# Cross-attention and gated feed-forward on one core: the last projections reordered over four PSUM banks, and the second group of first-layer weights loaded in the last units

## What is computed

```
x = x + tanh(g_xattn) * (attention(layer_norm(layer_norm(x)), ctx, mask) @ w_proj + b_proj)    # 16 heads of 32, 128 keys
x = x + tanh(g_ffn) * ffn(layer_norm(x))
ffn(h): y = silu(layer_norm(h) @ w1 + fc1_bias);  h + 0.5 * (y @ w2 + fc2_bias)                # 512 -> 2048 -> 512
w1 = (fc1_q - 128) * fc1_scales    (per group of 128 rows; w2 the same from fc2_q, fc2_scales)
```

## Time and profile before

| | |
|---|---|
| median of 3 runs | 1099.59 us (1096.32 to 1099.66) |
| the profiled execution | 1091.72 us, its span 1089.9 us |
| TensorE busy | 1030.1 us, 95% of the span |
| VectorE busy | 648.7 us, 60% |
| ScalarE, GpSimd busy | 398.8 us, 329.1 us |
| attention block | from 0 to 400.15 us |
| feed-forward block | from 400.15 us to the end |

### The profile page before, as it was taken

One profiled execution on the slowest core, in us unless ns is written; L12 is line 12 of the kernel. 1 busy time (PEld: TensorE's weight loads), 2 busy tenths in 40 slices (PEclk: granted clock), 3 DMA queues, 4 the chain that ended last, 5 costly groups with the idle time before them and its releaser, 6 DMA issues.

```text
span 1089.9 us, 15131 instructions
## 1 busy us (share of the span) xinstructions
PE 1030.1 (95%) x5182; PEld 561.6 (52%) x5182; DVE 648.7 (60%) x1071; ACT 398.8 (37%) x612; POOL 329.1 (30%) x338
## 2 busy tenths in 40 slices
PE   5787999999989797999999999999999999999998
PEld 3455767767767453444444444444444444444443
DVE  5678989889877767785344435335346345335322
ACT  3467777877767622341121121121121121121111
POOL 4456667667756332202101102102102102012000
PEclk9889999999999999999999999999999999999999
DMA  7575777777766679202002002001000100200101
GB/s 277 126 206 160 218 196 213 221 225 200 215 171 173 203 221 343 91 1 78 1 1 78 1 1 77 1 1 42 37 1 31 47 1 1 78 1 1 39 1 39
DMA packets 61473, 109.38 MB, mean 100 GB/s; under 512 B 9656, under 2 KB 10848, under 8 KB 60896
## 3 DMA queue, kind: packets, MB, share of 16 engines
q1 hardware_dynamic: 58632, 104.11, 31.4%
q10 hardware_dynamic: 2776, 4.40, 1.3%
HBM read 72.57 MB, written 33.55 MB: 97 GB/s over the span
## 4 chain that ended last, share of the span: by engine, by line
PE 57%; DVE 3%; issue 1%; DMA 1%; ACT 1%; DVEq 0%; SPq 0%
PE ps_z L1428 9%; PE ps_z L1427 9%; PE ps_z L1429 9%; PE ps_y L238 9%; PE ps_y L239 9%; PE ps_y L240 9%; PE ps_h L1441 1%; DMA s_raw<-in_L_ffn_fc_scales 1%; DVE w_f L192 1%; ACT w_hi L183 1%; DVE x_in L1521 0%; DVE y_hi L1490 0%; DVE w_lo L195 0%; DVE x_stats L1543 0%; DVE x L1513 0%
## 5 line engine op out<-in xcount | busy, mean ns | idle before, releaser
L1464 ACT ACTIVATE y_f<-ps_y,cols,ffn_scales 128x512 f32<-128x512 f32 x128 | 99.3, 776 | 490.3 <-PE ps_y L240 490.3
L1490 DVE TENSOR_SCALAR y_hi<-y_f,ffn_scales 128x512 f16<-128x512 f32 x128 | 70.1, 548 | 331.4 <-ACT y_f L1464 331.4
L1427 PE MATMUL ps_z<-w_hi,y_hi 128*128 128x512 f16 x512 | 194.8, 381 | 7.0 <-DVE w_lo L195 7.0
L238 PE MATMUL ps_y<-ht_hi,w_hi 128*128 128x512 f16 x512 | 194.1, 379 | 1.5 <-PEq L278 1.5
L1428 PE MATMUL ps_z<-w_lo,y_hi 128*128 128x512 f16 x512 | 194.8, 381 | 0.0
L1429 PE MATMUL ps_z<-w_hi,y_lo 128*128 128x512 f16 x512 | 194.6, 380 | 0.0
L240 PE MATMUL ps_y<-ht_hi,w_lo 128*128 128x512 f16 x512 | 194.1, 379 | 0.0
L239 PE MATMUL ps_y<-ht_lo,w_hi 128*128 128x512 f16 x512 | 194.1, 379 | 0.0
L1492 DVE SCALAR_TENSOR_TENSOR y_lo<-y_f,ffn_scales,y_hi 128x512 f16<-128x512 f32 x128 | 103.2, 806 | 4.6
L773 ACT ACTIVATE p_f<-ps_s,fill_col 128x512 f32<-128x512 f32 x128 | 86.2, 673 | 4.0 <-PE ps_s L604 3.5
L775 ACT ACTIVATE p_hi<-ps_s,fill_col 128x512 f16<-128x512 f32 x128 | 85.4, 667 | 0.0
(11 more groups left out here) (203 smaller groups left out, 1606.6 us busy)
## 6 DMA issues: line engine op xcount, KB each, us to landing
q_pack<-q_dram SPq DMA_DIRECT2D x96, 256.0 KB, 4.0
q_dram<-q_hi SPq DMA_DIRECT2D x32, 256.0 KB, 3.3
q_dram<-q_lo SPq DMA_DIRECT2D x32, 256.0 KB, 3.7
x_dram<-x_out SPq DMA_DIRECT2D x32, 256.0 KB, 4.8
x_res<-in_x SPq DMA_DIRECT2D x28, 256.0 KB, 4.7
q_raw<-in_L_ffn_fc_q SPq DMA_DIRECT2D x6, 1024.0 KB, 10.7
s_raw<-in_L_ffn_fc_scales SPq DMA_DIRECT2D x6, 1024.0 KB, 13.9
x_in<-in_x SPq DMA_DIRECT2D x4, 1024.0 KB, 7.7
```

The costliest lines, as they stand in the source:

```text
L238: nc.tensor.matmul(out, s_hi, m_hi, start=(k == 0), stop=False)
L1427: nc.tensor.matmul(ps_z[t][:, :], hi, w2_hi[:, f, :], start=(f == 0), stop=False)
L1464: nc.scalar.activation(y_f[f % 2][:, :], ps_y[f % 2][:, :], ACT.Silu, bias=b1_c[:, f:f + 1], scale=y_unscale).then_inc(y_f_ready, 1)
L1490: nc.vector.tensor_scalar(y_hi[f % 4][:, :], y_f[f % 2][:, :], y_scale, None, ALU.mult).then_inc(y_hi_ready, 1)
```

## The change

**Loads.** `load_w1(1)` moves from the SyncE queue at the start of `feed_forward` to the ScalarE queue in step 34 of attention, between `weights_hi(0, 0)` and `weights_hi(0, 1)`. For this the raw tiles have names by group, and the integers of groups 1 and 3 have a tile each (`q1_second`, `q1_last`).

**Projections.** In step 31 `project(26, first)`, and in step 32 both halves of tile 27, stand ahead of `weighted_values`. Tiles 28 to 31 have a bank each (`ps_xp`, `ps_qm`, `ps_s[0]`, `ps_s[1]`) and all run in step 33: four first halves, then four second halves. The sums of tiles 30 and 31 go to `xt_f` and not to `x1_out`.

```
+            q1_second = sb("q1_second", [P, KB, GROUP * P], I32, first)
...
+            s1_raw, q1_raw = [s1_even, s1_odd, s1_even, s1_odd], [q1_even, q1_second, q1_even, q1_last]
...
+        def summed(i, k):
+
+            return xt_f[k % 2][:, :] if last_tiles(i, k) and k % KB >= 2 else x1_out[k % 2][:, :]
+
         def proj_bank(i, k):
 
-            return ps_qm if not real(i, k + KB, UNITS) and k % 2 else ps_xp
+            return ps_xp if real(i, k + KB, UNITS) else (ps_xp, ps_qm, ps_s[0], ps_s[1])[k % KB]
...
-                    after(pe, x1_ready, tile if real(i, k + KB - 1, UNITS) else tile - 1)
+                    after(pe, x1_ready, tile if real(i, k + KB, UNITS) else UNITS - KB)
...
+                if isinstance(i, int) and PER * i + k >= UNITS - 1 and real(i, k - 5, UNITS - KB):
+                    project(i, k - 5, first)
+                if isinstance(i, int) and PER * i + k >= UNITS and real(i, k - 5, UNITS - KB):
+                    project(i, k - 5, second)
                 if real(i, k - 1, UNITS):
                     weighted_values(i, k - 1)
...
                 if real(i, k - 5, UNITS) and not real(i, k - 5 + KB, UNITS):
-                    if k % 2:
+                    if PER * i + k == UNITS + 1:
                         for blocks in (first, second):
-                            project(i, k - 5, blocks)
-                            project(i, k - 4, blocks)
+                            for t in range(KB):
+                                project(i, k - 5 + t, blocks)
                     return
...
+                if u == UNITS + 2:
+                    g("load_w1")(act, 1)
...
-                    load_w1(sp, 1)
```

More of the change, by code:

```diff
@@ L104, in build @@
         maxima = [sb(f"maxima{n}", [P, TT, HG], F32) for n in range(2)]
+        GROUP = 4
         ffn_scales = sb("ffn_scales", [P, D], F32)
@@ L112, in build @@
             xt_lo = [sb(f"xt_lo{n}", [P, KB, CHUNK], F32R, rows32) for n in range(2)]
[L116 to L119, removed]
+        ht_hi, ht_lo = [sb("ht_hi0", [P, KB, CHUNK], F16)], [sb("ht_lo0", [P, KB, CHUNK], F16)]
+        with ExitStack() as first:
+            q1_second = sb("q1_second", [P, KB, GROUP * P], I32, first)
+        ht_hi.append(sb("ht_hi1", [P, KB, CHUNK], F16))
+        ht_lo.append(sb("ht_lo1", [P, KB, CHUNK], F16))
         w_f = [sb(f"w_f{n}", [P, 2 * D], F32) for n in range(2)]
@@ L175, in w_parts @@
                 held = slice(2 * n % GROUP, 2 * n % GROUP + 2)
-                parts = [w2_hi[:, blocks, :], w2_lo[:, blocks, :], s2_raw[group % 2][:, held, :], q2_raw[group % 2][:, held, :]]
+                parts = [w2_hi[:, blocks, :], w2_lo[:, blocks, :], s2_raw[group][:, held, :], q2_raw[group][:, held, :]]
                 full = w_f[at % 2][:, :].rearrange("p (f d) -> p f d", f=2)
@@ L487, in step @@
                     after(sp, x1_ready, PER * i + tile + 1)
-                    sp.dma_start(target, x1_out[t % 2][:, :]).then_inc(x1_stored[t % 2], 16)
+                    sp.dma_start(target, summed(i, tile)).then_inc(x1_stored[t % 2], 16)
                 if k == -1:
@@ L677, in step @@
                 if real(i, k - 5, UNITS) and not real(i, k - 5 + KB, UNITS):
-                    if k % 2:
+                    if PER * i + k == UNITS + 1:
                         for blocks in (first, second):
-                            project(i, k - 5, blocks)
-                            project(i, k - 4, blocks)
+                            for t in range(KB):
+                                project(i, k - 5 + t, blocks)
                     return
-                if real(i, k - 5, UNITS):
+                if real(i, k - 5, UNITS) and not (isinstance(i, int) and PER * i + k >= UNITS - 1):
                     project(i, k - 5, first)
@@ L686, in step @@
                     scores(i, k, 2)
-                if real(i, k - 5, UNITS):
+                if real(i, k - 5, UNITS) and not (isinstance(i, int) and PER * i + k >= UNITS):
                     project(i, k - 5, second)
@@ L927, in add_residual @@
                 after(dve, res_biased, tile + 1)
-                if real(i, k - 2, UNITS):
+                if real(i, k - 2, UNITS) and not (last_tiles(i, k) and k % KB >= 2):
                     after(dve, x1_stored[k % 2], 8 * (tile - k % 2))
-                nc.vector.tensor_tensor(x1_out[k % 2][:, :], proj_bank(i, k)[:, :], residual(i, k), ALU.add).then_inc(x1_ready, 1)
+                nc.vector.tensor_tensor(summed(i, k), proj_bank(i, k)[:, :], residual(i, k), ALU.add).then_inc(x1_ready, 1)
             def row_stats(i, c, tiles=range(TT)):
```

24 lines of the change are left out of this document (12 added, 12 removed).

## The result

The changed kernel is slower by half a per cent, in line with the forecast:

| | median (range), us | runs | ratio to before, 95% interval |
|---|---|---|---|
| before | 1095.61 (1091.39 to 1099.66) | 12 | 1 |
| after | 1100.83 (1098.9 to 1105.75) | 12 | 1.0051 (1.0035 to 1.0068) |

A forecast was written before the change was run, and what follows sets the result against it. TensorE, busy 95% of the span, was taken as the bound; only its idle time could move. Terms 3.1 + 1.8 - 3.6 + 2.8 gave +4.1 us, 1103.7 against the median 1099.6; range 1098.0 to 1108.5.

The forecast's parts named there:

- The load saves 3.6 us: Start of feed-forward: VectorE's 3.58 us wait for the group 1 scales goes entirely; bounds 3.6 us and 0.
- 0 to 0.6 us, and I take 0: VectorE's wait for all stores ahead of its first `y_hi`: the loss from stores sharing DMA engines with the load.
- The halves ahead cost 3.1 us at tile 28: End of attention: projections ahead of the weighted values wait for additions, so tile 28 starts at 390.20, not 387.11.
- Predicted idle times: TensorE idles 3.0, 2.7, 3.5 and 3.7 us ahead of 372.12, 382.70, 390.20 and the feed-forward.
- 3.7 us: End of attention: net loss before load and later clock terms come off, +3.7 us, without any slow stretches in either kernel.
- The last stretch costs 1.8 us: Tiles 28 to 31: tile 29 completes after the 36th matmul, not the 24th, so the last addition ends 1.8 us later.
- The clock costs 2.8 us, two slow stretches of three: Tile 27, last projections, first hidden products: two of three get 1.2 GHz, 1.4 us each; bounds 0 and +4.2 us.
- Clock stays high: Rival: clock stays high behind the three later idle times, or drops behind one only: +1.3 to +2.7 us; chance 0.31.
- Halves fill the idle time: Rival: halves of tiles 26 and 27 fill TensorE's idle time, tile 28 starts 2.1 us sooner: -3.9 us; chance 0.05.
- The load brings nothing: Rival: VectorE waits as long for the load or another transfer: +7.7 us, 1107.3; chance 0.08.

The follow-up runs named there:

- the load alone: The kernel before with only the load of first-layer group 1 moved to step 34 of attention, projections as before: ratio 1.0018.
- Own banks: The changed kernel with tiles 26 and 27 projected into `ps_qm` and `ps_max[0]`, and tile 28 not waiting for tile 27's addition: ratio 0.9976.
- four banks alone: The kernel before with only tiles 28 to 31 over four banks and the last two sums in `xt_f`; load at its old place: ratio 1.0007.
- the filler: The changed kernel with 12 matmuls that nobody reads added behind the last projections: ratio 1.0038.
- the load with sums in `xt_f`: The kernel before with the load moved and the last two sums in `xt_f`; projections in pairs, no halves ahead: ratio 0.9967.
- the last three kernels: Own banks with both weight conversions ahead of the last four sums: half of tile 27 ahead, both halves, or both with tile 29's sum in `p_f[1]`: 0.9947, 0.9947, 0.9942.
- the last timeline: VectorE's rows for Own banks with both halves of tile 27 ahead and both weight conversions right behind tile 27's addition: ratio 0.9947.

## Why the prediction was right, and where it was off

**The load saves 3.6 us: right against the profile of before, wrong in what it needs.** The wait for the load went in every kernel with the load ahead. With the last sums out of `x1_out` and a fast start of the feed-forward the gain was 3.6 us (0.9967). By itself the load gained nothing (1.0018). The step that failed is "0 to 0.6 us, and I take 0" for the stores: I asked only whether VectorE's wait for all stores ahead of `y_hi` would grow, and not whether the additions would wait for a free `x1_out`. With the load alone they lost 2.30 - 1.05 + 3.77 = 5.0 us, of which 3.77 are shown to be the load's. In the changed kernel this stayed hidden, because its last two sums go to `xt_f` and its tile 29 comes late. The Trainium skill, DMA: Bandwidth & Descriptors (Issuing engines are not separate DMA queues), has the rule that was weighed there, that loads on ScalarE's queue run on the same 16 engines as the stores. The trace agrees: the store of tile 29 took 7.9 us to land beside the moved load, and 2.3 without it. A second thing the sum left out: it took the whole 3.58 us and a slow start of the feed-forward besides. The two hide each other. Where that start is slow, the wait for a load at its old place is only 1.14 or 1.17 us.

**The halves ahead cost 3.1 us at tile 28: right, 3.66 measured.** The mechanism stands row by row. Predicted idle times were 3.0, 2.7, 3.5 and 3.7 us; the trace has 2.95, 2.96, 3.48 and 3.65. `weighted_values(30)` start 4.37 us behind `p_lo` (3 to 4 were forecast), tile 28 at 393.60 less the 2.83 us of the ruler, 390.77, against 390.20. Own banks show that the bank wait is the cause: with it gone the same order of instructions starts `weighted_values(31)` 6.9 us sooner on the ruler, even 1.1 us ahead of the kernels without halves ahead. Across runs the cost is larger than 3.66. The four kernels of the table that stand without halves ahead and with shared banks have tile 28 at 14.9 to 15.0 us on the ruler, those with them at 20.1 to 20.3: 5.3 us. The profile of before had a slow stretch at tile 27 that they lack. The prediction named this ("3.7 us" without slow stretches) but didn't put it in the sum.

**The last stretch costs 1.8 us: right by itself (1.86), wrong as the worth of the edit.** (The 0.23 us between matmuls is 0.24 by the rows that it names, 11.22 us over 47; tile 29's addition starts 8.67 us behind tile 28's first matmul with four banks alone, where 8.5 were forecast.) "Four banks" held two things. The order costs; the sums in `xt_f` save, once the load slows the stores. Together they come to -3.8 us beside the load (1.0018 to 0.9983), and to -2.3 us beside load and halves (1.0072 to 1.0051); the intervals overlap in both pairs, a little in the first and over most of the narrower one in the second. The sums alone come to -5.6 us beside the load (1.0018 to 0.9967), and there the intervals are apart (from 0.9995, and up to 0.9982).

**The clock costs 2.8 us, two slow stretches of three: the count is right, the sizes are not.** Tile 27 kept the high clock. The last projections had 1.2 GHz from 395.1 to 398.1, which is 3.0 x (1 - 0.23 / 0.43) = 1.4 us, and 12.33 + 1.86 + 1.4 = 15.6 is the 15.63 of the ledger. The feed-forward's start cost 2.56 us and not 1.4, because its slow stretch went on from 410.0 to 415.5. Two experiments show this size apart from all else: 2.6 us with the filler, 2.6 us between the load alone and the load with sums in `xt_f`.

The sum on the ruler: 3.66 + (1.86 + 1.4) + 2.56 - 3.58 = +5.9, where the forecast had 3.1 + 1.8 + 2.8 - 3.6 = +4.1. Of the 1.8 us between them 1.2 are the clock at the feed-forward's start, and 0.6 the start of tile 28.

**Part of the agreement is luck.** This ledger is against one profile of before, with its slow stretch at tile 27. The kernels between before and after give the three moves one by one, on the ruler and in the timed runs:

| move | forecast, us | ruler, us | timed, us |
|---|---|---|---|
| four banks and the buffers of the sums | +1.8 | +0.4 | +0.8 |
| halves ahead, beside four banks, with their slow stretches | +3.1 + 2.8 = +5.9 | +6.9 | +8.2 |
| the load, beside both | -3.6 | -1.4 | -3.4 |
| sum | +4.1 | +5.9 | +5.6 |

The halves cost more than forecast and the four banks less, and these errors partly cancel. How much the load gives in the last place is not settled, since ruler and timed runs differ there by 2 us.

**The rivals.** "Clock stays high" (+1.3 to 2.7) is out: every profiled run with halves ahead in shared banks has the slow stretches at tile 26 and in the last projections. "Halves fill the idle time" did not happen in the changed kernel but did with own banks, and there its -3.9 us is near the measured -2.6 (-3.5 on the ruler) by luck: tile 28 gained 6.7 us against before and not 2.1, and VectorE's queue took 4.9 back, where 1.8 were forecast. "The load brings nothing" is true of the load alone, for a reason that the rival did not name, and not of the changed kernel.

## What to carry to other kernels

Before work is put into an engine's idle time, look up what that work itself waits for: a projection that needs the bank of the tile before waits behind the same `p_lo` that made the hole, and then holds up everything queued behind it. Give it a free bank, or leave it where it was.

A load that is moved ahead is paid by whoever uses the DMA engines at that time; look there for buffers that are reused as soon as they have been stored, and give the last ones buffers that needn't be. And when an engine has been freed, read who ends last now: here tile 28 came 6.7 us sooner than before, but only 1.8 of them reached the end of attention until VectorE's conversions were moved into its waits.

## What the hardware showed that I had not expected

**The clock at the feed-forward's start goes with the idle time ahead of it, in each of the 13 profiles.** TensorE idled 1.05, 1.54 and 1.54 us there with the filler, in before and with load, pairs and `xt_f`, and kept 2.4 GHz: 8.2 to 8.3 us from the last addition to the third conversion. In the other ten kernels it idled 3.00 to 6.64 us, fell to 1.2 GHz, and the same distance was 9.6 to 11.0 us, any wait for the load taken off. (In the last three kernels, with 9.6 to 9.8, it is a store that the first `y_hi` waits for last.) A wait of 3.77 us for a store, in the load alone, thus went with 2.6 us more behind it.

**But length alone does not decide.** In the changed kernel 2.95 us (to 374.95) went with the low clock and 2.96 us (to 385.93) did not.

**Conversions and GpSimd's additions lengthen each other.** The same `w_lo` takes 1.28 us, and 2.27 at 391.63 in the last timeline. GpSimd's timeline of that run, and of the run with own banks alone, whose conversions lie elsewhere:

```profile
389.29 3.52 POOL L1185 TENSOR_TENSOR p_f<-p_f,bp_rows 128x512 f32<-128x512 f32 x2
392.76 3.48 POOL L1185 TENSOR_TENSOR xt_f<-xt_f,bp_rows 128x512 f32<-128x512 f32 x2
```

```profile
391.18 2.53 POOL L1182 TENSOR_TENSOR p_f<-p_f,bp_rows 128x512 f32<-128x512 f32 x2
393.67 2.52 POOL L1182 TENSOR_TENSOR xt_f<-xt_f,bp_rows 128x512 f32<-128x512 f32 x2
```

`w_lo` takes about 1 us longer beside GpSimd's additions, and so does each pair of additions; `w_f` at 389.19, which started 0.1 us ahead of them, lost nothing. In the run with the load alone `w_f` did lose: started 0.24 us behind a GpSimd instruction (`o_lo`, at 389.25), it took 2.12 us, and GpSimd's next one 2.00, which takes 1.02 in the last timeline's run:

```profile
389.49 2.12 DVE L195 SCALAR_TENSOR_TENSOR w_f<-q_even,s_even 128x1024 f32<-128x1024 int32 x1
390.48 2.00 POOL L1225 TENSOR_TENSOR ln_s<-ln_a,expo 128x4 f32<-128x4 f32 x1
```

Where these rows show which of two started first, it is the second that takes longer. No run was made to test this.
